# Two stage boundaries of a one-core transformer kernel reworked: feed-forward work begun inside the first attention, and the tail begun on half of the samples

## What the reference computes

```
x = x + xattn0(ctx, layernorm(x))      # 16 heads, 256 x 77 scores, additive mask
x = x + ffn0(layernorm(x))             # 8-bit rows, ternary w1 (256->1024), 3-tap depthwise
                                       # convolution, silu, 8-bit rows, ternary w2 (1024->256)
x = x + xattn1(...)                    # second attention
x = x + ffn1(...)                      # self attention and a mixture of 8 experts
x = x + xattn2(...)                    # third attention
x = x + ffn2(layernorm(x))             # routed spline, below
x = x + gelu(layernorm(x) ctx^T) ctx   # feed-forward whose weights are the context
x = x + ffn3(layernorm(x))             # Hadamard rotation, 4-bit rows, ternary weight
```

```
def _calibrate(scores, knots, temperature):
    normalized = sigmoid(scores / (temperature[0] + 1e-06))
    idx_float = normalized * (K - 1)          # K = 8 knots, linear interpolation between them
    ...
```

## Time and profile before

| | us |
|---|---|
| median of three runs | 1222.53 |
| profiled execution, whole | 1223.4 |
| profiled execution, its span | 1221.7 |
| PE / DVE / ACT / POOL busy | 1115.7 / 766.5 / 431.7 / 524.0 |
| last projection matmul of att0 begins | 148.05 |
| first convolution of ffn0 begins | 162.84 |
| DVE begins `magnitudes(0)` | 1117.62 |
| DVE begins `curve(0)` | 1126.96 |
| DVE begins `mixed(0)` | 1140.48 |

### The profile page before, as it was taken

One profiled execution on the slowest core, in us unless ns is written; L12 is line 12 of the kernel. 1 busy time (PEld: TensorE's weight loads), 2 busy tenths in 40 slices (PEclk: granted clock), 3 DMA queues, 4 the chain that ended last, 5 costly groups with the idle time before them and its releaser, 6 DMA issues.

```text
span 1221.7 us, 20925 instructions
## 1 busy us (share of the span) xinstructions
PE 1115.7 (91%) x7456; PEld 934.8 (77%) x7456; DVE 766.5 (63%) x1737; ACT 431.7 (35%) x890; POOL 524.0 (43%) x499
## 2 busy tenths in 40 slices
PE   6899889998899988999987999999999799989895
PEld 4688768886577855889877999999997588865563
DVE  2687779998787735988862222222224888787683
ACT  2355432333455511111111222222222356562464
POOL 4454604446677321667757111100263665440342
PEclk9999989999899989799886999999999899997898
DMA  7999400000200020000034422211221100000001
GB/s 272 386 387 387 166 1 1 21 3 1 84 1 1 1 98 0 1 1 18 31 126 189 177 104 103 108 34 39 69 69 46 55 10 1 1 1 1 1 26 44
DMA packets 43733, 93.60 MB, mean 77 GB/s; under 512 B 3821, under 2 KB 17806, under 8 KB 40838
## 3 DMA queue, kind: packets, MB, share of 16 engines
q1 hardware_dynamic: 35254, 62.24, 14.1%
q0 software_dynamic: 7104, 29.14, 6.6%
q10 hardware_dynamic: 1296, 1.18, 0.3%
HBM read 39.02 MB, written 51.51 MB: 74 GB/s over the span
## 4 chain that ended last, share of the span: by engine, by line
PE 67%; DVE 18%; ACT 4%; issue 4%; POOL 4%; DMA 1%; POOLq 0%; DVEq 0%; SPq 0%; ACTq 0%
PE PS L2198 11%; PE PS L2208 10%; PE PS L1011 8%; PE PS L2075 4%; PE PS L1720 4%; PE PS L990 4%; PE PS L1024 3%; PE PS L980 3%; PE PS L2064 2%; PE PS L934 2%; DVE scr L1219 2%; PE PS L1424 2%; DVE scr L1245 2%; PE PS L2101 1%; DVE big L1213 1%
## 5 line engine op out<-in xcount | busy, mean ns | idle before, releaser
L2198 PEld LDWEIGHTS PS<-scr 128*128 128x128 f32 x992 | 118.3, 194 | 5.4 <-issue 1.7
L2198 PE MATMUL PS<-scr 128*128 128x128 f32 x992 | 120.5, 279 | 1.6 <-ACT scr L2226 1.3
L2231 ACT ACTIVATE scr<-PS,W 128x128 f32<-128x128 f32 x148 | 53.5, 367 | 192.8 <-PE PS L2198 192.8
L660 POOL TENSOR_TENSOR scr<-scr,small 128x1232 f32<-128x1232 f32 x32 | 71.8, 2245 | 107.1 <-DVE small L443 107.1
L2208 PE MATMUL PS<-scr 128*128 128x256 f32 x496 | 112.2, 379 | 0.0
L785 ACT ACTIVATE big<-PS 128x512 f32<-128x512 f32 x144 | 74.1, 524 | 88.2 <-PE PS L990 87.3
L2261 DVE TENSOR_SCALAR scr<-PS,W 128x128 f32<-128x128 f32 x148 | 51.3, 350 | 84.2 <-PE PS L2198 84.2
L2208 PEld LDWEIGHTS PS<-scr 128*128 128x128 f32 x496 | 91.8, 190 | 11.2
L2267 DVE TENSOR_TENSOR scr<-PS,W 128x256 f32<-128x256 f32 x37 | 15.7, 425 | 125.9 <-PE PS L2208 121.9
L990 PE MATMUL PS<-W,scr 128*128 128x128 f32 x480 | 79.9, 285 | 12.4 <-ACT big L763 3.0
L1011 PEld LDWEIGHTS PS<-scr,big 128*128 128x128 f32 x640 | 81.2, 191 | 6.8 <-issue 4.9
(11 more groups left out here) (410 smaller groups left out, 2516.1 us busy)
## 6 DMA issues: line engine op xcount, KB each, us to landing
expert_in<-zeros SPq DMA_DIRECT2D x1, 19712.0 KB, 55.8
expert_out<-zeros SPq DMA_DIRECT2D x1, 19712.0 KB, 107.0
scr<-ew_in POOLq DMA_DIRECT2D x12, 1024.0 KB, 6.4
scr<-expert_in SPq DMA_DIRECT2D x38, 128.0 KB, 2.1
big<-ew_in POOLq DMA_DIRECT2D x4, 1024.0 KB, 8.3
expert_out<-scr POOLq DMA_DIRECT2D x28, 128.0 KB, 2.0
W<-pack SPq DMA_DIRECT2D x1, 2458.0 KB, 8.7
W<-pack SPq DMA_DIRECT2D x1, 2152.0 KB, 9.6
```

Source lines behind the costliest of these rows:

```text
L660: g.tensor_tensor(sc3, sc3, a_mx[u % 3].unsqueeze(2).broadcast_to([P, H, S2]), ALU.subtract).then_inc(s["sub_ready"], 1)
L2198: ins = pe.matmul(bank(1 + f % 4, G), e_w1[slot][:, k, f * P:(f + 1) * P], e_xT[:, k, :], start=(k == 0), stop=(k == C - 1))
L2231: a.activation(e_h[:, f, :], bank(1 + f % 4, G), ACT.Relu, bias=moe_bias(e, f)).then_inc(s["h_act"], 1)
```

## The change

Site one, att0 and ffn0. The barrier behind att0 becomes `stage_left`. `weight_sum` works on half matrices in turns 3, 5, 7 and 9; PE adds the sums in turn 10; means, rounding of w1, quantization of sample 0 and rounding of w2 lie in turns 11 to 15; ACT takes the signs of w1 in turns 12 and 13; POOL makes the taps in turns 1, 7 and 9. PE transposes the quantized rows in turn 15 and makes the first two pairs of hidden channels in turn 16. The clearing of the second attention's blocks is cut in four and moved behind samples 1 to 4 of ffn0's POOL loop. Some buffers change their place.

Site two, att2 and tail. One exponential covers all 72 scores of a part, `calibrated` and `first_max` lose an instruction each to fused forms. Behind the loop DVE only chooses clusters for parts 1 and 2; the tile gates of samples 4 to 7 (`LATE = (8, 16)`) and `magnitudes(1)` lie in the tail's first turns. The Gelus lie together behind the loop, the last sample's hidden product has its own bank.

```diff
@@ att_dve, the loop over u
-                if lay == 0 and u in (14, 15):
-                    weight_sum(v, u - 14)
-                    ternary_stats(v, ch, u - 14)
+                if lay == 0 and u in (3, 5, 7, 9):
+                    weight_sum(v, (u - 3) // 4, (u - 3) // 2 % 2)
+                if lay == 0 and u == 10:
+                    ternary_stats(v, ch, 0)
+                if lay == 0 and u == 11:
+                    weight_means(v, ch)
+                if lay == 0 and u == 12:
+                    weight_rounded(v, 0)
+                if lay == 0 and u == 13:
+                    quant_rows(v, ch, 0)
+                    quant_largest(v, ch)
+                if lay == 0 and u == 14:
+                    quant_scales(v, ch)
+                    quant_rounded(v, ch)
+                if lay == 0 and u == 15:
+                    weight_rounded(v, 1)
+                    ternary_stats(v, ch, 1)
                 if lay == 0 and u == NT:
-                    weight_means(v, ch)
-                    weight_rounded(v, 0)
+                    borders(v, ch, slice(0, PAIRS))
+                    ch.sync()
+                    first_kept(v, 0, (0, 1))
...
                 if lay == 2 and u == 15:
-                    calibrated(v, ch, *PARTS[0], 1)
-                    first_max(v, ch, *PARTS[0], r_ohl)
+                    tile_calibrated(v, ch, *PARTS[0])
                 if lay == 2 and u == NT:
-                    tile_onehot(v, *PARTS[0])
+                    gate_args(v, 1)
+                    tile_chosen(v, ch, *PARTS[0])
...
                 row_stats(B - 1)
-                late_gates(v, ch, 1)
-                late_gates(v, ch, 2)
+                cluster_calibrated(v, ch, 1)
+                cluster_chosen(v, ch, 1)
+                gate_args(v, 2)
+                cluster_calibrated(v, ch, 2)
+                cluster_chosen(v, ch, 2)
+                compressed_dve(v)
@@ att_pool
+        TAPS_AT = {1: (0, 1, 2), 7: (3, 4, 5), 9: (6, 7)}
+                if lay == 0 and u in TAPS_AT:
+                    taps_made(g, TAPS_AT[u])
@@ att_act, behind the loop of lay 2
+                gate_exp(a, 1)
                 extra("rz", B - 2)
-                gate_exp(a, 2)
+                onehots_kept(a, 0, 0, 2)
                 row_normed(B - 1)
                 extra("rs", B - 2)
                 extra("rz", B - 1)
-                gate_exp(a, 3)
+                last_weights_act(a)
                 extra("rs", B - 1)
-                last_weights_act(a)
-                onehots_kept(a, 0)
-                gate_exp(a, 4)
-                compressed_act(a, EARLY, NT)
-                gate_exp(a, 5)
+                gate_exp(a, 2)
+                compressed_act(a, 0, NT // 2)
+                last_hidden_kept(a)
+                compressed_act(a, NT // 2, NT)
+                compressed_tanh(a)
@@ att_pe
+                if lay == 0 and u == NT:
+                    pe.wait_ge(ffn0["w_ready"], 2)
+                    pe.wait_ge(s["s_free"], S_FREE(0, NT - 1))
+                    first_made(pe, 0, 0)
                 if u >= 1:
                     turned(u - 1)
+                if lay == 0 and u == NT:
+                    first_made(pe, 0, 1)
...
+                if lay == 0 and u == NT - 1:
+                    pe.wait_ge(s["ring_free"], ...)
+                    quantized_turned(pe, 0)
@@ ffn0_pool
-            vb_zeroed(g, 1)
+            def second_zeroed(n):
+                part = a_VB[1][:, 5 * n // 2:5 * (n + 1) // 2, :, :, :]
...
+                if 1 <= i <= 4:
+                    second_zeroed(i - 1)
@@ tail_dve
-            magnitudes(0)
-            magnitudes(1)
+            magnitudes(0, 6)
+            tile_calibrated(v, ch, *LATE)
             curve(0)
             for j in range(B + 3):
                 if j < B:
                     curve_added(j)
+                if j == 0:
+                    tile_chosen(v, ch, *LATE)
                 if 1 <= j <= B:
                     mixed(j - 1)
                 if j + 1 < B:
                     curve(j + 1)
+                if j == 0:
+                    magnitudes(1, 5)
@@ tail_pe
-            pe.wait_ge(gates["onehot_ready"], 3)
-            onehots_turned(pe, range(6, 8), True)
-            parameters(pe, 1)
-            for n in range(2):
-                pe.wait_ge(*at("os_ready", n + 1))
-                onehots_turned(pe, range(4 * n, 4 * n + 4), True)
-                if n == 0:
-                    curve(0)
-                    curve(1)
+            pe.wait_ge(*at("os_ready", 1))
+            onehots_turned(pe, 0, 2)
+            clocked(pe, 5, 3)
+            curve(0)
+            curve(1)
+            clocked(pe, 5, 8)
@@ all four engines
             att_...(0)
-            stage_end(..., "att0")
+            stage_left(...)
```

More of the change, by code:

```diff
@@ L1470, in prepared @@
                     keys_made(pe, 1, i - 4, 5)
[L1472 to L1475 removed]
+            hidden(0, 2)
+            hidden(0, 3)
             pe.wait_ge(s["taps_ready"], FC)
```

440 lines of the change are left out of this document (247 added, 193 removed).

## The result

| | us |
|---|---|
| before, median of 20 runs | 1221.67 |
| after, median of 20 runs | 1219.44 (1213.38 to 1224.50) |
| ratio after / before | 0.9958, 95% interval 0.9939 to 0.9977 |
| forecast | 1206.5 (1198 to 1215) |

The change wins 0.4%, 5 us by the ratio (the medians alone differ by 2.2), where 16 were forecast. The gain is small, but both intervals leave out 1, here and on another chip, where the same two kernels gave 0.9963 (0.9941 to 0.9985). The time lies outside the forecast range.

A forecast was written before the change was run, and what follows sets the result against it. PE, busy 91% of the span, bounds the kernel; gains lie where it stands still or runs at the lower clock. 1223.4 - 9.8 - 6.5 = 1207.1 against the profiled execution, forecast as 1206.5 us, range 1198 to 1215.

The forecast's parts named there:

- First site: att0 to ffn0: first convolution 10.8 us earlier, less 1.0 for work moved into att0; net -9.8 us.
- the stretch of att0: Work moved into att0's turns: 1.0 us charged for turn 13, nothing for the others; bounds 0 and 4.
- Step 3: First site: from last projection to first convolution, projection 1.1 us plus two more hidden pairs 0.9.
- steps 1 and 2: First site: transposes in turn 15 and hidden products in turn 16 put the last projection 1.9 us later.
- wrong in kind: Condition the prediction set itself: it fails in kind if the loops between the sites change their length.
- Second site: att2 and tail: gates, compression, magnitudes and first curves sooner; net -6.5 us, bounds -10 and -2.
- step 1: Second site, gates: 15 instructions, 4.6 us, for 35 in 10.67; sample 7's scores left at 1102.5.
- step 4: Second site: DVE waits 3.0 us (2.2 to 5.1) for parameters before `magnitudes(1)`; `mixed(0)` 7.2 earlier.
- Step 5: Second site: one more block of transposes in turn 1, 0.7 us, on a full PE.
- the compression's products: Second site, step 2: eight tiny matmuls on PE behind the Gelus, 1.0 to 1.8 us.
- The second: Rival, tail: DVE waits for parameters on slow PE before `magnitudes(1)`, `mixed(0)` only 2 earlier: 1211.5 us; chance 0.14.
- The first: Rival: DVE and POOL block each other; 5 us lost in att0, 2 in ffn0's loop: 1213 us; chance 0.14.

The follow-up runs named there:

- e12: Kernel before with only the first site's edits (att0 and ffn0), run again on another chip: 1214.80 us, ratio 0.9928.
- e5: Kernel after, unchanged, measured again on another chip: 1218.98 us, ratio to before 0.9963.
- e1: Kernel before with only the first site's edits (att0 and ffn0): 1214.15 us, ratio 0.9883 beside a slower before.
- e4: Kernel after with 20 dummy matmuls for 8 on PE in front of the tail's first transposes: 1220.74 us, ratio 0.9934.
- e3: Kernel after with parameter products as before: one of 65 columns per block, partition halves in turn, two banks: 1215.57 us, ratio 0.9872.
- e10: Against e6: parameters of samples 4 to 7 behind sample 0's mixing product, `magnitudes(1)` one iteration later: 1208.83 us, ratio 0.9893.
- e7: Kernel after with DVE's row normalization using three tensor operands in place of one with two scalars: 1226.15 us, ratio 1.0026.
- e8: Kernel after with the edits of e3, e6 and e7 together: 1217.40 us, ratio 0.9950.
- e6: Against e3: tile choice of samples 0 to 3 moved behind the last residual and sample 7's statistics: 1211.20 us, ratio 0.9912.
- e13: Against e3: 16 parameter products with all of one partition half ahead of the other; one run, 1208.50 us, no ratio.
- e9: Against e6: first attention's row normalization moved ahead of its turn's scores, half sums of weights behind the residual: 1215.81 us, ratio 0.9947.
- e11: Edits of e9 and e10 together: 1210.65 us, ratio 0.9923.
- e14: Against e3: each parameter product split into 64 columns and 1, partition halves in turn; one run, 1221.17 us, no ratio.

## Why the prediction was wrong, point by point

**First site: right in size, in part by luck.** Forecast -9.8; e12 has 0.9928, which is -8.8 (-12.2 to -5.4). The convolution was to begin at 152.0, with the stretch of att0 at 153.0; it began at 153.9 and 154.3, in after at 155.15. Step 3 (projection to convolution 2.0) was 2.1. The last projection came at 151.8 and 152.2, 0.8 and 1.3 later than 150.95. Two terms were mis-sized, in opposite directions. The stretch of att0 was put at 1.0 in all. In turn 13 DVE's scores came 1.9 late, which put PE's projections back by 1.45, and "nothing for the others" was wrong by some 1.3, most of it from three pairs of L390 (2.82 for 2.31, as in the row at 110.68), each in a turn with POOL's taps: 2.8 in all. Against that, steps 1 and 2, the work added in turns 15 and 16, were put at 1.9 and cost 0.7 (e12: 4.68 and 3.88 between the last three projections, for 4.67 and 3.22 before). That the sum comes near is in part these two errors against each other. The ffn0 loop kept its length: first to last convolution 125.4 for 125.6.

**Between the sites** after lost 1.1 of 7.7 us, where the clock was 0.50 at 290 to 300. From the last convolution to DVE's first row maximum of the second attention it takes 25.9 us, in e5 25.8, in before, e1, e4 and e12 22.4 to 22.7; most of this comes back later. The prediction called itself wrong in kind if loops between the sites changed their length; no loop did by more than that, and the same code with a higher clock there (e4) did not.

**Second site: wrong, and mainly by one step.** The step that failed is the price of `parameters`, which stood twice in the sum. In step 1 ("one-hot transposes and parameters in front of it but two product matmuls less ... I leave it at 1102.5") it was nothing; PE spends 3.9 us on it, the scores came 5.3 late, and with the old form of the products they come 4.3 sooner (e3). In step 4 the queue of PE in front of `magnitudes(1)` was put at 6.2 at the lower clock with a wait of 3.0, bounds 2.2 to 5.1; the queue was 10.4 (1121.69 to 1132.1) and the wait 9.26. In e5 the wait was 5.37, still outside the bounds. The old price was that of 16 records in turn (1.1 us at full clock). The whole diff has a second product and another order, and I carried the old price over without counting. Added up: 5.3 late scores, 0.8 late compression, 6.3 wait, less 0.7 for the rest, are the 11.7 us between 40.3 and 52.0. e3 takes 9.9 of them back with this edit alone.

**Step 5 was too small as well.** It put one more block of transposes behind `mixed(0)` at 0.7 us. From `mixed(0)` to the last product it takes 75.4 to 75.5 us in before, e1 and e12, and 76.7 to 78.2 in the kernels with the second site's edits; the difference is there at the first ternary product. It is not the lower clock alone: e10 has full clock from 1115 to 1155 and takes 77.6. In after the block (0.66 on PE at 1147.54) and its copy (0.60 on ACT) stand in front of the next sample's work; the rest is open. This is why in e3 `mixed(0)` comes 5.4 sooner than before and the last product only 2.9. Even with cheap parameters (120.0 to 122.5 for 122.9) the tail wins 0.4 to 2.9 us, and with the 1.4 of the last attention that is less than the 6.5 forecast.

Smaller misses: the compression's products, put at 1.0 to 1.8, took 2.3 behind the second Gelu. Right in size: `magnitudes(0)` 2.7, `curve(0)` 7 behind its start (6.9), and with cheap parameters the wait of 3.0 (2.3) and 23.5 from `magnitudes(0)` to `mixed(0)` (23.4 in e3).

**The rivals.** The second ("gain taken back by the order of `magnitudes(1)`", 0.14) named the place and the mechanism, DVE waiting for parameters on a slow PE, but had `mixed(0)` still 2 us earlier than before, 5 less than forecast; on the scale of the table it came 4.5 later than before, 11.7 less. The first named the stretch of att0, which was 2.8 us, not 5, and none in ffn0's loop.

## What to carry to other kernels

Count the instructions that a function issues before and after the change, and their order, before taking the duration of the old one for it; here a product of one column was paid like one of 64. Ask of every block moved ahead on a busy engine what is queued behind it, and ask it at each call of a function that is called twice. Before explaining a loss by a wait in one profile, look for the same wait in a second profile of the same kernel: here it was 9.26 and 5.37. A stall beside another engine is not cured by moving the instruction if its input comes out of that engine's queue.

## What the runs showed of the hardware that was not expected

Times of after spread over 11 us, with mean granted clocks of 0.942 (1224.50) to 0.952 (1213.38). One place where they part is the pause of PE in front of L1047 at 140, which is 1.58 or 1.59 us long in twelve of the fourteen profiles that have the first site's edits (1.85 in e7 and e8). The granted clock from 140 to 150 was 1.00 in e1, e4, e6, e12 and e13, 0.83 in after, e5 and e10, and 0.63 to 0.67 in e3, e9, e11 and e14, which stayed at 0.50 to 0.52 until 160. The two windows of e3:

```profile
140.00:150.00 10.00, 9.33 (x50) 8.97 (x50) 6.90 (x18) 3.36 (x6) 2.88 (x3) 0.63 0.01 2
150.00:160.00 10.00, 9.64 (x42) 7.48 (x41) 2.94 (x8) 4.34 (x6) 0.00 (x0) 0.52 0.00 0
```

There the convolution began at 160.41, and most of the first site's gain was gone in that run. e6 has the same code up to this point, and its convolution began at 152.02. In the profile before the clock is 0.97 from 140 to 150, with all of PE's stop still to come. That the pause brings the lower clock on was not tested; the same pause stands in e6 and e12 without it, so the pause alone does not decide.
